# A state-space front end with its first units written out: weights loaded without a staging buffer, filter parameters made 32 steps at a time

## The reference, cut to what matters

```python
def reference(x, log_dt, B_ri, inv_A_real, A_imag, Wq, Wk, Wv, Wg, Wo, g_norm, W_gate, W_qkv):
    # tok: a state-space filter, H = 192 channels ("steps" below), N = 64 states, L = 512 outputs
    dt = exp(log_dt); A = -exp(inv_A_real) + 1j * A_imag; dtA = A * dt[:, None]
    C = (B * C_in) * (exp(dtA) - 1.0) / A               # C_in is the input x, (16, 192, 64) complex
    h = 2.0 * einsum('chn,hnl->chl', C, exp(dtA[:, :, None] * arange(512))).real   # (16, 192, 512)
    # attn: retention, 8 heads, on the normalized rows
    z = layernorm(h)
    q, k, v, g = rope(z @ Wq), rope(z @ Wk), z @ Wv, z @ Wg      # 512 -> 512, 512, 1024, 1024
    h = h + ((rmsnorm((q k^T * decay) v) * g_norm) * silu(g)) @ Wo
    # ffn: 16 heads of attention with keys and values of the top-1 head
    return h + gated_attention(layernorm(h), W_gate, W_qkv)
```

## Time and profile before

| | us |
|---|---|
| median of 3 runs | 1304.86 (1304.76 to 1305.59) |
| profiled execution | 1305.04 |
| its span, first to last instruction | 1303.3 |
| PE's first matmul | 43.33 |
| first projection of unit 0 | 63.26 |
| first projection of unit 1 | 91.30 |
| PE busy | 1208.9 (93%) |
| DVE / ACT / POOL busy | 723.5 / 563.5 / 520.1 |

### The profile page before, as it was taken

One profiled execution on the slowest core, in us unless ns is written; L12 is line 12 of the kernel. 1 busy time (PEld: TensorE's weight loads), 2 busy tenths in 40 slices (PEclk: granted clock), 3 DMA queues, 4 the chain that ended last, 5 costly groups with the idle time before them and its releaser, 6 DMA issues. The chain is left out here.

```text
span 1303.3 us, 22737 instructions
## 1 busy us (share of the span) xinstructions
PE 1208.9 (93%) x8176; PEld 991.1 (76%) x8176; DVE 723.5 (56%) x1360; ACT 563.5 (43%) x1777; POOL 520.1 (40%) x722
## 2 busy tenths in 40 slices
PE   0389999999999999789999999998999999999997
PEld 0368888888888888567778777787788787887875
DVE  7686655675765533265554545444564555645544
ACT  3344334444433421443433332324546455465556
POOL 2757667666766741143323333211312213122121
PEclk9999999999999999989999999998999999999999
DMA  4132222322222224985666645152443707336051
GB/s 157 61 127 98 105 105 93 118 89 113 106 96 115 90 97 158 307 226 158 198 172 202 194 139 145 50 119 54 88 94 70 161 12 154 82 83 138 10 130 34
DMA packets 63359, 154.78 MB, mean 119 GB/s; under 512 B 9616, under 2 KB 26128, under 8 KB 61712
## 3 DMA queue, kind: packets, MB, share of 16 engines
q1 hardware_dynamic: 63248, 153.33, 40.1%
HBM read 67.19 MB, written 56.62 MB: 95 GB/s over the span
## 5 line engine op out<-in xcount | busy, mean ns | idle before, releaser
L1692 ACT ACTIVATE probs<-psum,row_max 128x128 f32<-128x128 f32 (+1 forms) x384 | 143.0, 387 | 45.9 <-DVE row_max L1861 33.2
L1010 ACT ACTIVATE square_scratch<-psum 128x128 f32<-128x128 f32 x192 | 50.8, 275 | 173.9 <-PE psum L1244 173.9
L1861 DVE TENSOR_REDUCE row_max<-psum 128x2 f32<-128x384 f32 (+1 forms) x128 | 79.2, 619 | 71.8 <-PE psum L2098 42.1
L1992 POOL TENSOR_TENSOR h_rows<-h_rows,y_normed 128x512 f32<-128x512 f32 x24 | 30.7, 1281 | 213.7 <-DVE y_normed L1878 213.7
L1969 POOL TENSOR_TENSOR picked_rows<-picked_rows 128x768 f32<-128x768 f32 (+1 forms) x64 | 61.2, 957 | 104.3 <-DVE picked_rows L1843 100.5
L1184 POOL TENSOR_TENSOR rr<-ss,consts_r 128x3 f32<-128x3 f32 x64 | 13.4, 209 | 197.0 <-ACT square_scratch L1010 194.0
L712 PE MATMUL psum<-m,basis 128*128 128x64 f32 x384 | 48.9, 284 | 43.3 <-POOL basis L664 43.3
L683 POOL TENSOR_TENSOR stage<-stage 128x512 f32<-128x512 f32 x48 | 81.6, 1720 | 14.5 <-DVE stage L565 14.5
L1869 DVE COPY raw_f<-psum 128x512 f32<-128x512 f32 x64 | 44.2, 691 | 76.7 <-PE psum L2111 76.6
L712 PEld LDWEIGHTS psum<-m,basis 128*128 128x128 f32 x384 | 49.6, 203 | 45.3 <-issue 43.3
L1266 PE MATMUL psum<-wo_high,y_high 128*128 128x512 f32 x192 | 79.4, 414 | 1.8 <-issue 1.8
(11 more groups left out here) (272 smaller groups left out, 3527.3 us busy)
## 6 DMA issues: line engine op xcount, KB each, us to landing
qk<-stage SPq DMA_DIRECT2D x24, 512.0 KB, 2.6
v<-stage SPq DMA_DIRECT2D x24, 512.0 KB, 2.6
g<-gate_rows SPq DMA_DIRECT2D x24, 512.0 KB, 2.7
qk_rows<-qk SPq DMA_DIRECT2D x16, 512.0 KB, 7.4
q_stack_even<-q_t_high SPq DMA_DIRECT2D x32, 224.0 KB, 4.8
q_stack_even<-q_t_low SPq DMA_DIRECT2D x32, 224.0 KB, 6.6
q_stack_odd<-q_t_high SPq DMA_DIRECT2D x32, 224.0 KB, 5.1
q_stack_odd<-q_t_low SPq DMA_DIRECT2D x32, 224.0 KB, 6.7
```

The costliest lines, as they stand in the source:

```text
L1010: last = nc.scalar.activation(sqs[:, h % 2, t], psum[:, OB[h % 2], t * RV:(t + 1) * RV], ACT.Square, accum_out=ss[:, h % 2, t:t + 1])
L1692: last = nc.scalar.activation(pr[:, g % 2, c], psum[:, SB[g % 3], c], ACT.Exp, bias=mx[:, g % 3, x:x + 1], accum_out=dsum[:, t, h:h + 1])
L1861: V.reduce_max(mx[:, g % 3, 0:nh], psum[:, SB[g % 3], 0:nh * w].rearrange("p (h n) -> p h n", h=nh), AX, negate=True).then_inc(s_max.sem, 1)
L1992: G.tensor_tensor(h, h, yn[:, (NT * i + t) % 2].rearrange("p h f -> p (h f)"), ALU.add).then_inc(added.sem, 1)
```

## The change

The ramp and slot 0 are no longer special cases of `slots`: each engine has a function `first()` in which the work up to slot 0 is listed in its own order, and `slots` begins at 1 (SP: at -1). In detail:

- Each raw weight lies in its own tile, at the address of its low part (`w_raw`); all six loads are issued at once, no load waits. The order on SP is w0, c0, w1, identity, c1, w2, w3, rope table, w4, w5.
- ACT copies w0 after the trigonometry of chunk 0, and w1 to w5 after its digits. DVE splits w0 after the first row statistics, the others between its other work.
- The parameters are made in six groups of 32 steps (`GC`) with 24 operations each, five of them on two planes at once (64 columns). Group 0 in `first()`, group 1 in slot 1, groups 2 to 5 in slots 3, 7, 11 and 15, ahead of `rope`. `g4` holds two groups.
- For chunk 0 the corners, and for units 0 and 1 the basis adds, are DVE's. The rest stays with POOL, which waits for the group of its chunk (`GROUP_AT + GROUP_STEPS * (n + 1)`).
- The spectrum of unit 1 stands behind the first projection of unit 0, that of unit 2 behind the first projection of unit 1.

```diff
@@ tiles
-    w_pairs = [(sb(n + "_high", [P, KC, D], F32R), sb(n + "_low", [P, KC, D], F32R)) for n in names]
+    for n in names:
+        w_hi.append(sb(n + "_high", [P, KC, D], F32R))
+        with ExitStack() as under:
+            w_raw.append(under.enter_context(nc.sbuf_tensor(n + "_raw", [P, KC, D], F32)))
+        w_lo.append(sb(n + "_low", [P, KC, D], F32R))
...
-    g4 = sb("g4", [P, 4, T])
+    g4 = sb("g4", [P, 2, 4, GC])
@@ sync
         def load_w(n):
-            if n >= 2:
-
-                sp.wait_ge(w_high, n - 1)
-                sp.wait_ge(w_low, n - 1)
-            sp.dma_start(raw[:, n % 2], d["w_r"][n]).then_inc(w_in[n % 2], 16)
+            sp.dma_start(w_raw[n][:, :, :], d["w_r"][n]).then_inc(w_in[n], 16)
@@ scalar
+        def first():
+            trigonometry((0, 0))
+            w_copy(0)
+            digits((0, 0))
+            for n in range(1, NP):
+                w_copy(n)
+            k_evac((0, 0))
+            angle_size((0, 1))
+            h_evac((0, 0))
+            sines((0, 1))
+            norm((0, 0))
+            x_split((0, 0))
+            decay_exp((0, 1))
+            k_evac((0, 1))
+            digits((0, 1))
+            h_evac((0, 1))
+            norm((0, 1))
+            v_evac((0, 0), 0)
+            v_evac((0, 0), 1)
+            x_split((0, 1))
+            g_tanh((0, 0), 0)
@@ vector: a group (the same formulas as before on 32 columns; 24 steps)
+        def group(k):
+            cols = slice(k * GC, (k + 1) * GC)
+            if k >= 2:
+                dve.wait_ge(xy_ready.sem, chunk_at(xy_ready, (0, 2 * k - 3), 1))
+            step(V.tensor_tensor(x(0), ar, ar, ALU.mult))
...
+            step(V.tensor_tensor(both(5), both(4), bcast(b0, 1, 2), ALU.mult))
+            step(V.tensor_tensor(both(6), both(4), bcast(b1, 1, 2), ALU.mult))
...
+            assert n[0] == GROUP_AT + GROUP_STEPS * (k + 1)
@@ vector: slots
-            if even(u) and valid(step_of(u, 4)) and u[1] > -LEAD + 2:
+            if even(u) and valid(step_of(u, 4)):
                 reduce(chunk(step_of(u, 4)))
...
             if valid(step_of(u, 1)):
                 row_stats(step_of(u, 1))
+            if u[1] % 4 == 3 and valid(step_of(u, 5)):
+                group((u[1] + 5) // 4)
             if valid(u):
                 rope(u, 0)
                 rope(u, 1)
+            if u == (0, 1):
+                scale((0, 2))
+                group(1)
+                x_split((0, 2))
             if valid(step_of(u, 3)):
                 build(step_of(u, 3))
...
+        def first():
+            group(0)
+            scale((0, 0))
+            corners(dve, V, (0, 0))
+            build((0, 0))
+            basis_add(dve, V, (0, 0))
+            reduce((0, 1))
+            row_stats((0, 0))
+            dve.wait_ge(rstd.sem, rstd.of((0, 0), 1))
+            split_weights(0)
+            x_split((0, 0))
+            build((0, 1))
+            basis_add(dve, V, (0, 1))
+            split_weights(1)
+            scale((0, 1))
+            split_weights(2)
+            split_weights(3)
+            dve.wait_ge(const_in, 32)
+            row_stats((0, 1))
+            rope((0, 0), 0)
+            build((0, 2))
+            split_weights(4)
+            rope((0, 0), 1)
+            split_weights(5)
+            x_split((0, 1))
+            build((0, 3))
+            gates((0, 0), 0)
+            reduce((0, 2))
@@ gpsimd
+            if u == (0, 2):
+                corners(pool, G, c)
+                scales((0, 1))
...
+        def first():
+            decay((0, 0))
+            moving((0, 0))
+            decay((0, 1))
+            moving((0, 1))
+            scales((0, 0))
+            moving((0, 2))
+            basis_add(pool, G, (0, 2))
+            rope_add((0, 0), 0)
+            rope_add((0, 0), 1)
+            moving((0, 3))
+            basis_add(pool, G, (0, 3))
+            decay((0, 2))
@@ tensor: slots
-            if valid(nxt):
+            if u == (0, 1):
+                spectrum(nxt)
+            elif valid(nxt):
                 row_transposes(nxt)
...
+        def first():
+            u, nxt = (0, 0), (0, 1)
+            spectrum(u)
+            row_transposes(u)
+            x_transposes(u)
+            pe.wait_ge(x_low.sem, x_low.of(u, 1))
+            project(u, WQ, 0).then_inc(qk_sum.sem, 1)
+            spectrum(nxt)
+            project(u, WK, 1).then_inc(qk_sum.sem, 1)
+            row_transposes(nxt)
+            project(u, WV, 2).then_inc(v_sum.sem, 1)
...
```

More of the change, by code:

```diff
@@ L40 @@
 HCH = 16
+GC = 2 * HCH
 NCH = T // HCH
@@ L46 @@
 NU = T // HALF
-LEAD = 4
 NP = 6
@@ L175, in stage_p @@
     const_in = sem("const_in_p")
-    w_in = [sem(f"w_in{q}") for q in range(2)]
+    w_in = [sem(f"w_in{n}") for n in range(NP)]
     w_high = sem("w_high")
@@ L247, in even, with slots, corners, basis_add @@
         return u[1] % 2 == 0
-    def slots(slot):
-        for n in range(-LEAD, NU + 1):
+    def slots(slot, first):
+        for n in range(first, NU + 1):
             slot((0, n))
+    def corners(eng, E, c):
+        q = c[1] % 2
+        co, si = cs[:, q, :, NB0 + NB1:NL], sn[:, q, :, NB0 + NB1:NL]
+        eng.wait_ge(scaled.sem, chunk_at(scaled, c, 1))
+        n, hs = c[1] // 2, slice(q * HCH, (q + 1) * HCH)
+        eng.wait_ge(par_dve, GROUP_AT + GROUP_STEPS * (n + 1))
+        g = lambda k: bcast(g4[:, n % 2, k, hs], 2, NA)
+        E.tensor_tensor(xyt[:, 0], g(0), co, ALU.mult)
+        E.tensor_tensor(xyt[:, 1], g(1), si, ALU.mult)
+        E.tensor_tensor(xyt[:, 2], g(2), si, ALU.mult)
+        E.tensor_tensor(xyt[:, 3], g(3), co, ALU.mult).then_inc(xy_chain.sem, 1)
+        eng.wait_ge(xy_chain.sem, chunk_at(xy_chain, c, 1))
+        E.tensor_tensor(xy[:, q, 0], xyt[:, 0], xyt[:, 1], ALU.add)
+        E.tensor_tensor(xy[:, q, 1], xyt[:, 2], xyt[:, 3], ALU.add).then_inc(xy_ready.sem, 1)
+    def basis_add(eng, E, u):
+        f = u[1] % 2
+        eng.wait_ge(v_ready.sem, v_ready.of(u, 1))
+        flat = lambda x: x.rearrange("p h y x -> p (h y x)")
+        E.tensor_tensor(flat(pc[:, f]), flat(pc[:, f]), flat(qs[:, f]), ALU.add).then_inc(basis_sum.sem, 1)
     def sync(sp, prefetch, prefetch_more):
@@ L428, in slot @@
                 digits(chunk(step_of(u, 4)))
-        slots(slot)
+        def first():
[19 more added lines that the diff above has]
+            g_tanh((0, 0), 0)
+        first()
+        slots(slot, 1)
     def vector(dve):
@@ L443, in vector @@
         aim, br, bi = prm[:, 2, :], prm[:, 3, :], prm[:, 4, :]
-        tn, sh, ch = tmp[:, 0, :], tmp[:, 1, :], tmp[:, 2, :]
-        t = lambda k: tmp[:, k, :]
+        tn, sh, ch = halves[:, 0], halves[:, 1], halves[:, 2]
+        t = lambda k: angle_tmp[:, k]
         dve.wait_ge(par_act, 1)
@@ L478, in vector @@
[L478 to L489, removed]
@@ L694, in slot @@
                 moving(step_of(u, 3))
-                basis_add(step_of(u, 3))
-        slots(slot)
+                basis_add(pool, G, step_of(u, 3))
+        def first():
[11 more added lines that the diff above has]
+            decay((0, 2))
+        first()
+        slots(slot, 1)
     def tensor(pe):
@@ L768, in slot @@
                 project(u, WG + 1, 5).then_inc(g_sum.sem, 1)
-        slots(slot)
+        def first():
[7 more added lines that the diff above has]
+            project(u, WK, 1).then_inc(qk_sum.sem, 1)
+            row_transposes(nxt)
+            project(u, WV, 2).then_inc(v_sum.sem, 1)
+            project(u, WV + 1, 3).then_inc(v_sum.sem, 1)
+            x_transposes(nxt)
+            pe.wait_ge(roped.sem, roped.of(u, 1))
+            project(u, WG, 4).then_inc(g_sum.sem, 1)
+            pe.wait_ge(roped.sem, roped.of(u, 2))
+            project(u, WG + 1, 5).then_inc(g_sum.sem, 1)
+        first()
+        slots(slot, 1)
     end = (0, NU - 1)
```

174 lines of the change are left out of this document (81 added, 93 removed).

## The result

The changed kernel took 1297.26 us (median of 4 runs, 1295.52 to 1298.30), against 1304.81 for the kernel before in the same comparison: ratio 0.9943, 95% interval 0.9927 to 0.9958. The forecast was 1294, range 1285 to 1302. The gain is 7.5 us where 11 were forecast. The profiled execution took 1297.08, span 1295.3.

The account below looks back on a forecast made before the run. PE is busy 93% of the span, so only its idle time, all before unit 1, can be won. 25.3 - 1.7 - 10.2 - 2.0 = 11.4 us off 1304.86 gives 1293.5, rounded to 1294; range 1285 to 1302.

Parts of the forecast that it names:

- The opening: Start up to unit 1: first matmul at 27.5, first projection at 40.9, unit 1 at 66.0, 25.3 us earlier.
- (a): One spectrum that stood before unit 1's start now stands behind it: 1.7 us given back.
- (c): Parameter group 1 on DVE ahead of POOL's corners: spectrum 4 3.0 us late, unit 3's projection 1.1; with (b) 10.2.
- (d): Groups 2 to 5, in units 3, 7, 11, 15, push POOL's work into the next angle reduction: 0.5 each, 2.0 us.
- The 32 us for a halved pace: Opening: if the load pace halved, the rope table would land at 32 us, 4 late, instead of 20.
- R4: No change at the end: first matmul waits for the table or next stage absorbs the shift; 1299 to 1305, chance 0.08.
- (b): POOL late before spectrum 3: PE waits 4.3 us, and 1.8 more at the lower clock level.
- POOL's ten operations: Moving operands, basis adds and rope adds from 56.9 us: 14.1 us alone, 21 beside DVE's work, ending at 78.0.
- the late waits: PE's waits behind unit 1's start, before spectra 3 and 4 and unit 3's projection: 4.3, 3.0 and 1.1 us.
- R1: The late waits don't come, since DVE and POOL hold each other less or at other moments; 1282 to 1285, chance 0.18.
- 2 to 3 named as a sign: Sign expected in the changed profile: a second PE idle of 2 to 3 us, before spectrum 4.
- R2: Opening won, but POOL and DVE later in units up to 4, groups 1.1 or more each; 1299 to 1301, chance 0.18.

Follow-up runs that it names:

- a: Changed kernel with parameter groups 2 to 5 ahead of the row statistics on DVE, not after them: 1291.09 us.
- b: Changed kernel with parameter groups 2 to 5 behind the two basis products on DVE: 1312.30 us.
- f: Changed kernel with parameter group 1 left out, one operation copying group 0's values in its place: 1293.34 us.
- g: As a, with parameter group 1 cut in three, 10 of its steps moved to earlier places where DVE idles: 1289.41 us.
- e: Changed kernel with the six corner products of chunk 0 back on POOL: 1298.17 us.
- i: As e, with splits 0 and 1 back among the first basis products and the first two basis adds back on POOL: 1304.87 us.
- j: Changed kernel with ScalarE's copies of the last two gate weights ahead of unit 0's x copy: 1299.82 us.

## Why the prediction was right, and which term was too small

By the end of P the parts add up to 25.2 - 12.1 - 6.3 = 6.7 us (520.29 against 527.01), where the forecast had 25.3 - 11.9 - 2.0 = 11.4. The opening and the sum of (a) to (c) came as forecast, (d) did not. The range held; the narrower 1290 to 1297 that had the chance 0.50 was missed by 0.3.

**The opening.** The 24 steps took 5.97 us (12.70 to 18.67; forecast 5.5 to 6.0), the first matmul came at 27.44 (27.5), the first projection at 41.25 (40.9), unit 1 at 66.14 (66.0). The row copy waited for the Abs (34.32), the table and later weights were hidden. (The 32 us for a halved pace in the prediction is a wrong sum: the 17.4 us of loading from 2.6 on would become 34.9 and end at 37.5. R4 alone rests on it, the 1294 does not.) Unit 1 was 25.2 us earlier, on record 25.3. In unit 0 the waits were 1.44, 0.74 and 1.11 for 2.1, 1.0 and 1.2.

**(a), (b) and (c).** From unit 1 to unit 3 the kernel before took 38.4 us and the changed one 50.5: 12.1 given back, on record 1.7 + 10.2 = 11.9. That the sum is so close is luck: two errors cancel. The waits are 4.16, 1.49 and 0.91 = 6.6 for 4.3 + 3.0 + 1.1 = 8.4; the lower clock and the restarts are the other 3.9 (12.1 less 1.7 and 6.6), for 1.8. Behind spectrum 3 the matmuls start 0.43 us apart until 85.71, in place of 0.23. POOL's ten operations are as forecast. The timeline of the changed kernel:

```profile
56.91 3.11 POOL L728 TENSOR_TENSOR mt<-cin,xy 128x512 f32<-128x512 f32 x1
59.98 1.05 POOL L729 TENSOR_TENSOR mt<-cin,xy 128x512 f32<-128x512 f32 x1
61.11 3.21 POOL L734 TENSOR_TENSOR m<-mt 128x512 f32<-128x512 f32 x1
64.28 3.37 POOL L280 TENSOR_TENSOR basis<-basis 128x1024 f32<-128x1024 f32 x1
67.62 3.88 POOL L753 TENSOR_TENSOR stage<-stage 128x512 f32<-128x512 f32 x2
...
75.40 2.72 POOL L280 TENSOR_TENSOR basis<-basis 128x1024 f32<-128x1024 f32 x1
```

From 56.91 to 78.12 is 21.2 us (21 on record, 14.1 alone; the two rows that the prediction names would give 15.1, and 14.1 comes out, to 0.1, with the products' 1.06 us at 142.34 and 143.36 of the same trace). Spectrum 3 starts at 77.9 to 78.3 in the changed kernel, a, b, f and g, though unit 1 starts anywhere from 66.14 to 67.86 in these: POOL sets it, not PE. That the late waits did come excludes R1. The wait before spectrum 4 was 1.49, under the 2 to 3 named as a sign.

**(d), the mis-sized term.** "Its bounds are 0 and, with the scaling slowed as well, 1.1 each; I take 0.5, so 2.0." From unit 3 to the end of P the kernel before took 397.3 us, the changed one 403.6: 6.3, or 1.6 for each group. That is 4.3 more than 2.0, and 1293.5 + 4.3 = 1297.8 is what was measured but for 0.5. PE's last gate projection therefore came some 6.7 us earlier and not 10 to 12, the sign on record. The mechanism was the one on record. DVE's timeline behind group 2, chunk 4:

```profile
137.39 0.62 DVE L518 TENSOR_TENSOR ang<-w,consts_a 128x448 f32<-128x448 f32 x1
138.04 1.35 DVE L519 TENSOR_SCALAR turn<-ang 128x448 f32<-128x448 f32 x1
139.43 2.47 DVE L520 TENSOR_SCALAR turn<-turn 128x448 f32<-128x448 f32 x1
...
152.91 1.29 DVE L530 TENSOR_TENSOR sin_cos<-sin_cos,mag 128x448 f32<-128x448 f32 x1 [1.12 <-ACT mag L370]
154.13 1.71 DVE L531 TENSOR_TENSOR sin_cos<-sin_cos,mag 128x448 f32<-128x448 f32 x1
155.76 0.68 DVE L614 TENSOR_TENSOR x_low<-psum,x_high 128x512 fp32r<-128x512 f32 x1
```

The same two scaling products in the kernel before:

```profile
162.16 0.63 DVE L521 TENSOR_TENSOR sin_cos<-sin_cos,mag 128x448 f32<-128x448 f32 x1 [0.80 <-ACT mag L340]
162.71 1.49 DVE L522 TENSOR_TENSOR sin_cos<-sin_cos,mag 128x448 f32<-128x448 f32 x1
```

The reduction took 7.5 us (137.39 to 144.93), as I had it, 3.6 more than alone. But the scaling was slowed too, 1.29 and 1.71 for 0.63 and 1.49: 0.9 more. 4.5 against a slack of 3.2 is 1.3, and PE waits 1.24. This case was named as the bound and not taken. What no bound had is the restart: a group of four units takes 78.09 us (156.50 to 234.59) and without waits 4 times 19.14 = 76.56 (19.14 is half of 129.72 to 168.00 in the kernel before), so each wait of 1.24 costs 1.53. The matmul behind the wait shows 0.50 us for 0.39. The choice of 0.5 between 0 and 1.1 was where the forecast went wrong; R2 had 1.1 or more each, but its other half, 3 to 5 us more in the units up to 4, did not come. a and b show the cause: with all four waits gone a takes 397.4 us from unit 3 to the end of P, as the kernel before does (by the end of P it gains 5.1, since its unit 3 starts 1.1 later), and b takes 420.2.

**The rule behind it.** The Trainium skill (SBUF — State Buffer, Who interferes with whom) says that of DVE, with two SBUF inputs, and a GpSimd instruction that reads SBUF, one blocks the other for the whole instruction. The runs agree: 0.30 against 2.28 us for the same operation in e and i. By the same section a DVE instruction with at most one SBUF input, outside its two-port modes, does not contend; the rope products read one of their inputs from PSUM, and the last two take 0.41 us beside POOL's rope add, as the two at 128.26 and 128.59 do beside an idle POOL:

```profile
129.09 3.52 POOL L753 TENSOR_TENSOR stage<-stage 128x512 f32<-128x512 f32 x2 [5.84 <-DVE stage L629]
129.52 0.41 DVE L628 TENSOR_TENSOR stage<-psum,rope_tables 128x256 f32<-128x256 f32 x1
129.85 0.41 DVE L629 TENSOR_TENSOR stage<-psum,rope_tables 128x256 f32<-128x256 f32 x1
```

Not only operations with two inputs are held: L519 and L520 of the reduction above have one tensor input and take 1.35 and 2.47 us beside POOL, against 0.39 each in b at 142.30 and 142.73, where POOL is idle.

## What to carry to other kernels

When two engines exclude each other, an added operation costs by its place: list what the other engine has queued beside it, and put it where that engine, or its own, waits for something else anyway. A start won at the opening is worth only what the first late chain behind it lets through; add up that chain's lone times and one foreign operation for each of its own. A short stall that comes back with each period is to be priced at its upper bound plus the restart: here that would have been 1.4 a group, and 1.6 was measured.

## What the runs showed of the hardware

- After an idle of 2.50 us before the gate projection, f's matmuls took 0.63 us each from 61.06 until 63.62, that is at the lower of the two clock levels. After 1.97 us before spectrum 4 in j they took 0.63 from 107.11 to 109.67; after 1.49 at the same place of the changed kernel they took 0.40. I had priced the low clock for the long wait alone.
- The clock comes back at different moments in runs of the same instructions: the first projection's matmuls are at 0.63 until 44.83 in the changed kernel and to the last one (46.10) in f, with the same start (41.25, 41.23). A difference of 1 to 1.5 us in one profile there means nothing by itself.
- A chained DVE operation over 32 columns takes 0.19 us and starts 0.22 to 0.23 after the one before; the reciprocal takes 0.35 at 32 columns and 1.35 at 192, 6.3 ns a column, against about 1 ns for the others.
